# A decoder layer on one core: three of twelve context chunks weighed by fp32r products of halves instead of float32 products

## The reference

```
x = x + gaussian_self_attention(layernorm(x))        # 20 LSTM cells give the centre and width of each token's window
x = x + cross_attention(layernorm(x), ctx, ctx)      # 16 heads of 64:
    q = (Q @ WQ).reshape(N, ql, 16, 64); k, v likewise from ctx
    weights = softmax(einsum('nqhk,nlhk->nhql', q, k) / sqrt(64), axis=3)
    attn = einsum('nhqk,nkhv->nqhv', weights, v)
    return attn @ WO + bO
x = x + moe_ffn(layernorm(x))                        # 4 experts, argmax routing, exact gelu, layernorm
```

## Time and profile before

| | |
|---|---|
| median of 3 runs | 1571.7 us (1571.29 to 1578.18) |
| the profiled execution's own time | 1573.7 us |
| its span | 1571.9 us |
| TensorE busy | 1515.6 us (96%) |
| VectorE busy | 1123.9 us (71%) |
| ScalarE busy | 905.5 us (58%) |
| GpSimd busy | 792.8 us (50%) |
| periods in the trace | (0,0) from 176.8; (7,0) from 757.60 to 797.27; (7,1) from 797.27 to 840.23; (14,0) ends at 1376.82 |

### The profile page before, as it was taken

One profiled execution on the slowest core, in us unless ns is written; L12 is line 12 of the kernel. 1 busy time (PEld: TensorE's weight loads), 2 busy tenths in 40 slices (PEclk: granted clock), 3 DMA queues, 4 the chain that ended last, 5 costly groups with the idle time before them and its releaser, 6 DMA issues.

```text
span 1571.9 us, 25217 instructions
## 1 busy us (share of the span) xinstructions
PE 1515.6 (96%) x7579; PEld 1094.0 (70%) x7579; DVE 1123.9 (71%) x1816; ACT 905.5 (58%) x1238; POOL 792.8 (50%) x407
## 2 busy tenths in 40 slices
PE   6988999999999999999999999999999999999897
PEld 3446667777777777777777777777777777777485
DVE  4338785868686878778786868686868686987756
ACT  4235675656666666666566666566656666665421
POOL 2002374555556565656555555555555556665611
PEclk9997998999999999999999999999999999999999
DMA  4100010100000000000000000100000000110000
GB/s 154 37 6 15 1 40 38 40 29 38 27 37 30 38 39 39 39 39 39 39 39 39 39 39 39 39 39 35 37 27 38 27 37 33 40 40 20 0 1 24
DMA packets 15251, 54.92 MB, mean 35 GB/s; under 512 B 1111, under 2 KB 6314, under 8 KB 15214
## 3 DMA queue, kind: packets, MB, share of 16 engines
q1 hardware_dynamic: 15214, 54.46, 9.2%
HBM read 53.54 MB, written 0.92 MB: 35 GB/s over the span
## 4 chain that ended last, share of the span: by engine, by line
PE 81%; DVE 9%; ACT 5%; issue 3%; POOL 1%; DMA 0%; DVEq 0%; POOLq 0%; ACTq 0%
PE ps L735 33%; PE ps L701 27%; PE ps L591 3%; PE ps L596 3%; PE ps L582 3%; DVE arena L1300 3%; PE ps L575 3%; PE ps L794 2%; ACT arena L992 2%; PE ps L715 2%; PE ps L511 1%; POOL arena L443 1%; ACT arena L892 1%; PE ps L723 1%; ACT arena L894 1%
## 5 line engine op out<-in xcount | busy, mean ns | idle before, releaser
L1286 DVE TENSOR_TENSOR arena<-arena,ps 125x896 f32<-125x896 f32 x336 | 363.4, 1081 | 98.4 <-PE ps L701 98.1
L443 POOL TENSOR_TENSOR arena<-arena,ring 125x896 f32<-125x896 f32 x192 | 417.6, 2175 | 17.4
L701 PE MATMUL ps<-q_hi,ctxT_hi 128*125 128x448 f32 x768 | 400.5, 522 | 2.5 <-ACT arena L986 1.0
L443 POOL TENSOR_TENSOR arena<-arena 125x896 f32<-125x896 f32 x112 | 236.8, 2114 | 316.2 <-ACT arena L992 307.2
L735 PE MATMUL ps<-ring,ctx_nat 125*128 125x448 f32 x768 | 345.3, 546 | 0.0
L986 ACT ACTIVATE ring<-ps 125x896 f32<-125x896 f32 x192 | 176.5, 919 | 238.9 <-PE ps L735 149.4
L701 PE MATMUL ps<-q_hi,ctxT_lo 128*125 128x448 f32 x768 | 281.7, 367 | 0.0
L701 PE MATMUL ps<-q_lo,ctxT_hi 128*125 128x448 f32 x768 | 281.6, 367 | 0.0
L735 PE MATMUL ps<-arena,ctx_nat 125*128 125x448 f32 x576 | 242.9, 544 | 2.4
L1300 DVE TENSOR_TENSOR ring<-ring,ps 125x896 f32<-125x896 f32 x192 | 201.6, 1078 | 0.0
L701 PEld LDWEIGHTS ps<-q_hi,ctxT_hi 128*125 128x125 f32 x768 | 144.2, 188 | 64.3 <-issue 47.3
(11 more groups left out here) (204 smaller groups left out, 1926.8 us busy)
## 6 DMA issues: line engine op xcount, KB each, us to landing
ctx_raw<-in_ctx_dram SPq DMA_DIRECT2D x32, 750.0 KB
ctx_nat<-in_ctx_dram SPq DMA_DIRECT2D x32, 750.0 KB
w_sb<-in_L_ffn_W_dram SPq DMA_DIRECT2D x1, 1024.0 KB
resid<-in_x_dram SPq DMA_DIRECT2D x1, 896.0 KB, 6.2
out_dram<-ctx_raw SPq DMA_DIRECT2D x4, 224.0 KB, 2.5
ctx_raw<-in_L_xattn_WQ_dram SPq DMA_DIRECT2D x1, 512.0 KB
w_sb<-in_L_xattn_WK_dram SPq DMA_DIRECT2D x1, 512.0 KB
w_sb<-in_L_xattn_WV_dram SPq DMA_DIRECT2D x1, 512.0 KB
```

The lines of the kernel that those rows point to most:

```text
L443: g.tensor_tensor(summed, chunk[0] if j == 1 else summed, chunk[j], ALU.add).then_inc(s["prob_added"], 1)
L701: m = mm(score_ps[j % 2][:, half, :], cx[k][:, rows], q[k][:, cols], start=(n == 0), stop=(n == 2))
L1286: v.tensor_tensor(run_max, kept(k, 0) if j == 1 else run_max, score_ps[j % 2], ALU.max).then_inc(s["maxed"], 1)
```

## The change

In every period but (15,1), the chunks 7, 9 and 11 are weighed by three fp32r products for each half: context high x probability high, context low x probability high, context high x probability low. The other nine chunks stay float32.

- GpSimd makes both halves of those three context chunks (`context_halves`: 125 x 384 elements, two operations) for the next period, after the weighing of the current one is complete and before its first addition.
- ScalarE makes the high half of the probabilities (`high_probability`, 125 x 896): chunk 7's in slot 5, ahead of the exponentials of chunks 10 and 11; chunk 9's at the start of slot 8 and chunk 11's at the start of slot 10, each after the weighing of the split chunk before it, as there is one `p_hi`.
- VectorE makes the low half (`low_probability`, 125 x 896) in the slot before the weighing, right behind `run_maximum`.
- TensorE's split weighing is two products for half 0, the side piece, two for half 1, then the two with the low half.
- To make room, `xnorm` is laid over the late ring buffers and over the space of `wT_sb`, and `rows_b` goes into the arena; `scale(3, q)` waits for the transposes of the tile whose place it takes.

```diff
+    SPLIT = (7, 9, 11)
+    NS = len(SPLIT)
...
-        xnorm = sb("xnorm", [TOK, PAIRS, D])
+        p_hi, p_lo = [sb(name, [CR, 2, HALF], F32R) for name in ("p_hi", "p_lo")]
+        ctx_hi, ctx_lo = [sb(name, [CR, NS, D], F32R) for name in ("ctx_hi", "ctx_lo")]
...
+        def split_chunks(i, k):
+            return () if isinstance(i, int) and i == PAIRS - 1 and k == 1 else SPLIT
+        def split_count(b, j):
+            return NS * b + SPLIT.index(j) + 1
+        def halves_free(b, j):
+            n = SPLIT.index(j)
+            return CH * b + (SPLIT[n - 1] + 1 if n else 0)
... GpSimd
+            def context_halves(i, k):
+                nb = 2 * i + k
+                chunks = slice(SPLIT[0], SPLIT[-1] + 1, SPLIT[1] - SPLIT[0])
+                need(pool, f"nat_in{k}", 16 * (i + 1))
+                need(pool, "weighted", CH * nb)
+                g.tensor_tensor(ctx_hi[:], ctx_nat[k][:, chunks, :], ones[0:CR, None, :].to_broadcast((CR, NS, D)), ALU.mult).then_inc(s["ctx_hi_done"], 1)
+                need(pool, "ctx_hi_done", nb + 1)
+                g.tensor_tensor(ctx_lo[:], ctx_nat[k][:, chunks, :], ctx_hi[:].bitcast(F32), ALU.subtract).then_inc(s["ctx_lo_done"], 1)
... at the end of GpSimd's period
+                if not (isinstance(i, int) and i == PAIRS - 1):
+                    context_halves(i + k, 1 - k)
... TensorE, weigh
+                if j in split_chunks(i, k):
+                    n = SPLIT.index(j)
+                    if half == 0:
+                        if n == 0:
+                            need(pe, "ctx_lo_done", b + 1)
+                        need(pe, "prob_hi_done", split_count(b, j))
+                    for cx in (ctx_hi, ctx_lo):
+                        mm(usum_ps[:, half, :], cx[:, n, :], p_hi[:, half, :], start=False, stop=False)
+                    if half == 1:
+                        need(pe, "prob_lo_done", split_count(b, j))
+                        for part in range(2):
+                            m = mm(usum_ps[:, part, :], ctx_hi[:, n, :], p_lo[:, part, :], start=False, stop=(j == CH - 1))
+                else:
... ScalarE
+            def high_probability(b, k, j):
+                need(act, "prob_done", step_count(b, j))
+                need(act, "weighted", halves_free(b, j))
+                a(p_hi[:], kept(k, j), ACT.Copy).then_inc(s["prob_hi_done"], 1)
... ScalarE, period
+                    if j > SPLIT[0] and j + 1 in split_chunks(i, k):
+                        high_probability(b, k, j + 1)
                     if j:
                         side_copies(i, k, j - 1, (1, 2, 3))
                     side_copies(i, k, j, (0,))
                     if j and not last:
                         keep_scores(b + 1, 1 - k, j)
+                    if j == SPLIT[0] - 2 and split_chunks(i, k):
+                        high_probability(b, k, SPLIT[0])
                     for n in EXPS_AT.get(j, ()):
... VectorE
+                if count == 3:
+                    need(dve, "xT_ps", 2 * GROUPS + q - 1 if q > 1 else 0)
...
+            def low_probability(b, k, j):
+                need(dve, "prob_hi_done", split_count(b, j))
+                v.tensor_tensor(p_lo[:], kept(k, j), p_hi[:].bitcast(F32), ALU.subtract).then_inc(s["prob_lo_done"], 1)
... VectorE, period, behind run_maximum
+                    if j + 1 in split_chunks(i, k):
+                        low_probability(b, k, j + 1)
```

More of the change, by code:

```diff
@@ L120, in decoder_layer @@
         ring.append(wo_raw[0:CR].rearrange("p f n -> p (f n)")[:, 0:HQ].rearrange("p (a b) -> p a b", a=2))
-        ring += [sb(f"ring{n}", [CR, 2, HALF])[:] for n in range(len(ring), CH)]
+        late_ring = sb("late_ring", [128, (CH - len(ring)) * HQ])
+        ring += [late_ring[0:CR, n * HQ:(n + 1) * HQ].rearrange("p (a b) -> p a b", a=2) for n in range(CH - len(ring))]
+        xnorm_first = late_ring[0:TOK, 0:PAIRS * D].rearrange("p (k d) -> p k d", k=PAIRS)
         first_odd = x_halves[0:CR].bitcast(F32).rearrange("p (a b) -> p a b", a=2)
@@ L171, in decoder_layer @@
         wv_raw = w1_sb[:].rearrange("p e f -> p (e f)")[:, H * DK:2 * H * DK]
-        wT_sb = sb("wT_sb", [128, 2, 3, D])
+        turned_space = sb("turned_space", [128, 2 * G4 * D])
+        wT_sb = turned_space[:, 0:6 * D].rearrange("p (a n d) -> p a n d", a=2, n=3)
+        xnorm_last = turned_space[0:TOK].rearrange("p (n k d) -> p n k d", n=2, k=G4)
         at[0] = 0
@@ L177, in decoder_layer @@
         yT_sb = [cut(GT) for n in range(2)]
+        rows_b = cut(2 * D, TOK).rearrange("p (n d) -> p n d", n=2)
         seen = sb("seen", [TOK, PAIRS])
@@ L236, in decoder_layer, with normed @@
         EXPS_AT = {0: (2, 3), **SUBS_AT}
+        def normed(count, t):
+            return xnorm_first[:, t, :] if count < 3 else xnorm_last[:, t // G4 % 2, t % G4, :]
+        def split_chunks(i, k):
[5 more added lines that the diff above has]
+            return CH * b + (SPLIT[n - 1] + 1 if n else 0)
         def step_count(b, j, half=1):
@@ L430, in _ @@
                 power(2, q)
+            def context_halves(i, k):
[6 more added lines that the diff above has]
+                g.tensor_tensor(ctx_lo[:], ctx_nat[k][:, chunks, :], ctx_hi[:].bitcast(F32), ALU.subtract).then_inc(s["ctx_lo_done"], 1)
+            context_halves(0, 0)
             def period(i, k):
@@ L668, in self_attention @@
                 for t in range(G4):
-                    m = mm(ps[0:TOK, SELF_BANK[q], t * D:(t + 1) * D], gauss_wT[:, G4 * q + t, :], xnorm[:, G4 * q + t, :], start=True, stop=True)
+                    m = mm(ps[0:TOK, SELF_BANK[q], t * D:(t + 1) * D], gauss_wT[:, G4 * q + t, :], normed(1, G4 * q + t), start=True, stop=True)
                 m.then_inc(s["self_attn_ps"], 1)
@@ L732, in weigh @@
                         need(pe, f"nat_in{k}", 16 * (i + 1))
-                if half == 0 or j == 0:
-                    need(pe, "prob_done", step_count(b, j, half))
-                m = mm(usum_ps[:, half, :], ctx_nat[k][:, j, :], kept(k, j)[:, half, :], start=(j == 0), stop=(j == CH - 1))
+                if j in split_chunks(i, k):
[11 more added lines that the diff above has]
+                else:
+                    if half == 0 or j == 0:
+                        need(pe, "prob_done", step_count(b, j, half))
+                    m = mm(usum_ps[:, half, :], ctx_nat[k][:, j, :], kept(k, j)[:, half, :], start=(j == 0), stop=(j == CH - 1))
                 if half == 1:
```

9 lines of the change are left out of this document (4 added, 5 removed).

## The result

The changed kernel is slower: 1597.9 us median of 4 runs (1596.5 to 1598.6), against 1571.6 before (1571.3 to 1578.2). The ratio is 1.0154, with an interval of 1.0139 to 1.0169. The forecast was 1558, and 1571 was the upper end of its range. The span of the profiled execution is 1596.8 us, 24.9 more.

A forecast was written before the change was run, and what follows sets the result against it. TensorE was taken to set the pace, with VectorE right behind. Gains of 16.1 us in pairs 1 to 13, small terms elsewhere and -4.9 in (14,0) made 13.3 us: 1558 us forecast, range 1547 to 1571.

The forecast's parts named there:

- The bound, and the split chunk: TensorE sets the pace, VectorE right behind; six products of 0.204 us replace 1.51 us of weighing, saving 0.28 a chunk.
- 0.189: Rival, chance 0.06: each split product on TensorE takes this many us, its lower bound, giving 1552 us in all.
- Chunk 11 gives almost nothing: At a period's end TensorE waits for VectorE's last maximum, so only 0.03 (k=0) or 0.09 us (k=1) of 0.28 is kept.
- The subtraction of 1.00 us, hidden: VectorE's three low-half subtractions per period cost 1.00 us each, at most 1.42, and fit without delaying TensorE.
- The eight rows of 1.08: Trace rows of the query's low half on VectorE, used to price the subtraction at 1.00 us rather than 1.42.
- It fits with 0.4 us to spare: In (7,0), chunk 9's subtraction goes between VectorE's additions at 785.10 and 789.12: 3.65 of 4.02 us used.
- free in slot 6: Chunk 7's subtraction on VectorE costs nothing: it moves the turned low half up to 1 us, with over 1 in hand.
- VectorE takes over the k=0 periods: Rival, chance 0.16: subtractions cost 1.42 us beside GpSimd, so k=0 periods outgrow VectorE's room; 1565 to 1570 us.
- ScalarE's copies, TensorE's waits: In the loop, three ScalarE copies of 0.94 us per period and TensorE's three added waits per split chunk cost nothing.
- GpSimd's halves hidden: Two GpSimd operations of 1.05 us each before a period's first addition, under 5.9 us of cover, cost nothing.
- (14,0) and (14,1): Late periods: (14,0) loses 4.9 us through three subtractions on late VectorE and a possible clock fall; (14,1) gains 0.65.
- The clock rival: Rival, chance 0.10: in slots 9 to 11 of k=1 periods the clock falls to 0.50, 4.8 us each, up to 1625.

The follow-up runs named there:

- e11: e9 with period (0,0) left as in the kernel before, no chunk split in it: 1564.7 us, 0.9946 of the kernel before.
- e1: Changed kernel without VectorE's subtraction: TensorE takes the high half again in the fifth and sixth product, without waiting for a low half: 1568.5 us, 0.9978 of before.
- e9: e5 with the query's low half of k=0 moved to the end of slot 8, and chunks 9 and 11 split in k=1: 1571.3 us, 0.9984 of before.
- e10: e5 with only the query's low half of k=0 moved to the end of slot 8, chunks 9 and 10 split: 1572.1 us, 0.9985 of before.
- e3: Changed kernel with GpSimd's additions of probabilities cut to the first query of each head, all subtractions kept: 1564.4 us, 0.9934 of before.
- e7: Changed kernel with the subtraction ahead of its slot's running maximum and its second operand read from the score bank in PSUM: 1580.7 us, 1.0032 of before.
- e5: Changed kernel with chunks 9 and 10 split, pairs 0 to 13 only, low halves moved toward GpSimd's gaps, first halves made later: 1586.5 us, 1.0059 of before.
- e2: Kernel before with GpSimd's additions of probabilities cut to the first query of each head: 1567.9 us, 0.9964 of before.

## Why the prediction was wrong

**The bound, and the split chunk: right.** TensorE set the pace with VectorE right behind it, and three-pass weighing is 1.21 us in the chain of the changed kernel and 1.23 in that of e11. e1 gives 0.56 and 0.55 us for (7,0) and (7,1), which is chunks 7 and 9 at 0.28 each. The product of 0.204 was right; neither 0.189 nor a dearer one showed.

**Chunk 11 gives almost nothing: right.** The 0.56 and 0.55 us leave nothing for it; I had 0.03 and 0.09. This is most of the difference between 16.1 and 13.7 us. e9 and e10 show it directly: their k=1 periods split chunks 9 and 11, and 9 and 10, and take 42.69 and 42.39 us, against 42.96 before: with 9 and 11 the period gains what chunk 9 alone is worth.

**The subtraction of 1.00 us, hidden: this is the step that failed.** I took 1.00 as its price and 1.42 as its upper bound, from the query's low half. The price is 1.0 us plus what is left of the operation that GpSimd has begun, up to 2.58 us in all in this kernel, and a second operation of VectorE behind it pays as well, with 3.01. I had read the 1.42 as "beside GpSimd", and still took it for the end of a range rather than one draw of a wait that can be as long as an addition. The eight rows of 1.08 were no evidence for new places: in k=0 that low half runs when the additions are over (33.6 of the period, the last addition ends at 30), and in k=1 it starts 0.04 us ahead of one and wins. "It fits with 0.4 us to spare" in the stretch of rows 3 and "free in slot 6" both fell with it: 21.3 us in the loop (e3 against the changed kernel), which turned 13.2 gained into 8.1 lost. (The four terms of that stretch add up to 3.64, not 3.65, which changes nothing.)
The Trainium skill has this rule ("SBUF — State Buffer", on the two separate sides of SBUF): VectorE and GpSimd share a pair of ports as an exclusive lock, taken by a VectorE instruction in a two-port mode, or by one with two SBUF inputs, the latter only against a GpSimd instruction that reads SBUF; whichever starts first keeps it to its end. The traces agree in each point that they touch: the subtraction ends 0.95 to 1.00 us after the addition, the addition takes 3.00 where it is second, and e7's operand in PSUM is never held up. By that rule, as an estimate with the 2.11 us of the earlier trace rows, each subtraction put beside the additions costs up to 2.1 us more, which points to a loss where I had a gain.

**The rival "VectorE takes over the k=0 periods"** was the nearest (0.16, 1565 to 1570), but for a price of 1.42, and it left the k=1 periods out, where the loss is greater.

**ScalarE's copies, TensorE's waits: right.** The copies are 942 ns, and e3, which has them and all three waits, gains 13.2 us in the loop.

**GpSimd's halves hidden: wrong at the two ends.** They are 1.00 us each, near the 1.05 of the scaling, and no engine's wait in the trace ends on them. But they too shut VectorE's scalings out, for 2.0 us before the first period and 1.5 in (14,0), and I had both at nothing. A cover in GpSimd's own queue says nothing of what its work does to VectorE.

**(14,0) and (14,1): too small by more than half, and wrong in cause.** I had 4.9 us lost for (14,0) with the clock's fall behind it, and 0.65 gained in (14,1). Measured are 4.3 lost in (14,0) and 5.8 in (14,1). In (14,1) the granted clock is 0.50 for its first 5.3 us and for 3.4 more from 1424.2, which accounts for up to 4.4 us. The cause that I named for (14,0), three subtractions of VectorE, is the lesser part: e1 without any subtraction still loses 3.7 there. Of these 1.5 are the scalings, and 0.8 the turned low half that waits for ScalarE's copy (22.8 in place of 21.9 of the period), as predicted; the rest I did not take apart.

**The clock rival** did not come in the changed kernel's loop, whose clock is 1.00 from 270 to 1349. It did come in e5 and e10, at the very place named but with chunk 10 split, at 3.2 us a fall and not 4.8.

**Where the distance to the forecast is.** The forecast had 13.3 us gained, and the profiled execution shows 24.9 lost, 38.2 apart. The loop has 24.2 of them (21.3 by the held-up subtractions), (14,0) and (14,1) 5.9, the part before the first period 5.0, pair 0 1.9 and the end 1.2.

**Left open.** Of the 5.0 us before the first period 2.0 are the scalings. The other 3.0 are there before the scalings begin: the first of the second layer norm starts at 144.52 us, against 141.56. That start lies between 140.87 and 144.70 over the thirteen kernels, one execution each, and the latest is e2's, which up to there has the same instructions as the kernel before. So these 3.0 us are as large as what one execution differs from another, and I can't put them down to the change. The clock is at 0.5 in other places of that part in every trace, and I did not separate it.

## What to carry to other kernels

Before an operation is given to VectorE, look at what GpSimd does at that time, and at the operation's operands: with both in SBUF it costs its own time plus the rest of whatever GpSimd has begun, and the operation behind it can pay as well. Read the partner's durations too: additions of 3.0 us among many of 2.1, one in nearly every k=1 period, were the sign of it in the kernel before. Place such operations in GpSimd's gaps or give them an operand in PSUM, and count only the saving of chunks whose end is not another engine's.

## What the runs showed of the hardware

- Subtraction of 125 x 896, both operands in SBUF: 1.08 us alone; started during an operation of GpSimd it ends 0.95 to 1.00 us after that one does (up to 2.58 us, 43 of 93 in the changed kernel). With one operand in PSUM: 1.086 mean of 78, beside additions as well (e7).
- The exclusion works both ways: GpSimd's addition of 2.11 us takes 3.00 when the subtraction was first by 0.07 us.
- VectorE's scaling with one SBUF tensor and two columns of scalars meets it as well: eight of 112 x 128 in 3.62 and 4.35 us in place of 2.13 and 2.35, beside GpSimd's halves, and one in 2.24 us in place of 0.34 beside an addition (kernel before, 1406.27).
- The granted clock fell to 0.5 in stretches where TensorE never idled but took sums of one column and split products in turn (e5, e10), for 6.8 us each, at a cost of 3.2 us.
